# Weights of the FFN built piece by piece inside chunk 0, and the values of chunk 1 emptied by DVE: an attention and FFN layer on eight cores

## The chip, the cores and the metric

The kernel runs on one Trainium2 chip, with the same program on all 8 of its cores. Each core takes 4 of the 32 batch entries, and the cores exchange nothing. The time is that of the slowest core in device microseconds, and a figure for a kernel is the median of its runs.

## The reference, cut to what matters

```python
xn = layernorm(x)                                # x: 32 x 2048 x 1024
q1, q2, k1, k2 = (xn @ W.T for W in (W1_q, W2_q, W1_k, W2_k))   # 16 heads x 4
L_q, L_k = exterior(q1, q2), exterior(k1, k2)    # 6 products per head, unit norm
scores = (L_q @ (L_k @ J6.T).T) * 6 ** -0.5      # causal, softmax over the keys
out = softmax(scores) @ (xn @ W_v.T + b_v)       # 16 heads x 64
attn = out @ W_out.T + b_out
W_real = einsum('abcd,cefg->abefdg', G1_R, G2_R).reshape(512, 512)   # 4 terms
W_imag = einsum('abcd,cefg->abefdg', G1_I, G2_I).reshape(512, 512)
ffn = [x_re @ W_real.T - x_im @ W_imag.T, x_re @ W_imag.T + x_im @ W_real.T] + bias
return x + attn + ffn                            # x_re, x_im: the halves of xn
```

## The kernel before

A core has 8192 rows of x: 64 tiles of 128 rows, 4 tiles to a chunk, 16 chunks, 4 chunks to a batch entry. All engines run their instructions in the order of the program, which is written out by this Python code, so the place of a call is the place in every queue that it touches.

**Start-up (L707 to L741).** Tiles 0 to 3 are normalised and transposed on PE, their query and key products are made, then `v_unit(t, 0, True)` makes the first half of their values. A `v_unit` (L409) is 32 matmuls into the one bank F (L281), and then an eviction of F: with `by_act` true by ACT (L423), otherwise by DVE (L430). `evicted` (L285) notes who frees F and calls `background()`. For tiles 4 to 7 the layernorm comes in pieces from `ln_pipeline` (L672): `first` is the statistics on DVE (L212, L213), `second` is 1/std on ACT (L220, L222) with the statistics of the next tile, `third` is the application on DVE (L229), which in the start-up is followed by the transposes on PE (L245) and a copy by ACT (L256). One `background()` call stands ahead of the second halves of the values, `v_unit(t, 1, True)`, and each of these four calls it again when it has evicted.

**Background work.** Three queues hold pieces: `ext` (exterior products and norms of a new chunk's queries and keys: L338 to L380 on DVE, with `rsqrt` on ACT, L361), `lns` (the layernorm two chunks ahead) and `ffn`. The last has 24 pieces, `ffn_pieces` (L512): for each of 8 blocks of the FFN weights `products` (L519), `pairs` (L526) and `total` (L532, in the imaginary half with the negated copy L536). The one `background()` makes `pieces_at_once` rounds, and a round takes a piece of the first non-empty queue of `ext`, `lns`, `ffn`, in that order; a piece that puts nothing on DVE lets the round go on to the next queue. `pieces_at_once` is 2 at the end of the start-up, 3 in chunk 0 and 1 after it. Applying layernorm off PE sends a DMA transpose and the load of a later tile through SP's queue (L238, L207), and the last exterior piece four DMA transposes (L393, L396).

**The loop over chunks (L841).** A chunk's steps are pairs of a head group (4 of 4 heads) and a key tile `kt`; chunk 0 has 16 steps, each with `scores` on PE (L596), `exps` on ACT (L607), for diagonal tiles a `mask` on DVE (L617), and two steps later `sums` on PE (L635). A head group ends with `reciprocals` on ACT (L646, L648) and `normalize` on DVE (L656). Between them `Fillers.work` runs units on PE up to a quota: in chunk 0 two `qk_unit`s and eight `v_unit`s of chunk 1, each of 8 work units, and then `bias_unit` (L542, 32 matmuls of L559 in two halves; it makes the constant `outb`, L570, then loads the residual tiles 0 and 1, to which GpSimd adds `outb`, L451). In later chunks there are `out_unit`s (L491) too, the first users of the FFN weights: they make the FFN and the output projection of the chunk before, and DVE adds F to the residual (L483). All these units share bank F, so each waits for the eviction of the one before. At the end of a chunk what is left of `ext`, `lns` and `ffn` is issued in one go.

Of the kernel before, what the change touches and what calls it, by code (L numbers as in the profile page):

```python
# [19 lines left out]
CH = 4  # L20
# [37 lines left out]
def build(nb=NB):  # L58
# [22 lines left out]
    with st:  # L81
# [74 lines left out]
        xb_in = {}  # L156
# [3 lines left out]
        def wait_for(eng, token):  # L160
            if token is not None:
                token[0].wait(eng, token[1])
# [122 lines left out]
        def evicted(token):  # L285

            f_free[0] = token
            background()
# [190 lines left out]
        def out_add(t, half, bank):  # L479
            tS.wait(VE, tS.n)  # L480
            gS.wait(VE, xb_in[t])
            r = residual(t)[:, half * 512:half * 512 + 512]
            return vS.inc(VE.tensor_tensor(r, bank, r, OP.add))  # L483

        def store(t, half):

            cols = slice(0, 1024) if half is None else slice(half * 512, half * 512 + 512)
            vS.wait(SY, vS.n)
            y_out[t] = d_y[t % 2].inc(SY.dma_start(y_d[t * 128:(t + 1) * 128, cols], residual(t)[:, cols]), 16)

        def out_unit(t, half):  # L491
            wait_for(TE, f_free[0])
            yield from out_products(t, half, F, range(4), True)
            n = out_add(t, half, F[:])
            if half == 1:
                store(t, None)
                if t + 2 < NT - CH or t + 4 == NT - 1:
                    later.append(lambda: load_xb(t + (2 if t + 2 < NT - CH else 4)))
            evicted((vS, n))
# [12 lines left out]
        def ffn_pieces(ri, j):  # L512


            w = (wr, wi)[ri][:, j * 512:(j + 1) * 512]

            def products():
                d_g2.wait(VE, d_g2.n)
                vS.inc(VE.tensor_tensor(fview(TERM, [[512, 4], [16, 32], [1, 16]]),  # L519
                                        fview(G1O + (ri * 4 + j) * 128, [[32, 4], [1, 32], [0, 16]]),  # L520
                                        fview(G2O + ri * 64, [[16, 4], [0, 32], [1, 16]]), OP.mult))
                return True

            def pairs():
                vS.wait(VE, vS.n)
                vS.inc(VE.tensor_tensor(fview(TERM + 2048, [[1, 1024]]), fview(TERM, [[1, 1024]]),  # L526
                                        fview(TERM + 1024, [[1, 1024]]), OP.add))
                return True

            def total():  # L530
                vS.wait(VE, vS.n)
                vS.inc(VE.tensor_tensor(w, fview(TERM + 2048, [[1, 512]]), fview(TERM + 2560, [[1, 512]]),  # L532
                                        OP.add))
                if ri == 1:
                    vS.wait(VE, vS.n)
                    vS.inc(VE.tensor_scalar(wn[:, j * 512:(j + 1) * 512], w, -1.0, None, OP.mult))  # L536
                ffn_in[0] = vS.n
                return True

            return [products, pairs, total]  # L540
# [39 lines left out]
        def in_pairs(c, kt):  # L580


            return c % NCH >= 2 and shape(c, kt) < 256
# [76 lines left out]
        ext = deque()  # L660
        lns = deque()
        ffn = deque()
        later = deque()
        pieces_at_once = [1]

        def background():
            for _ in range(pieces_at_once[0]):
                for lane in [lane for lane in (ext, lns, ffn) if lane]:
                    if lane.popleft()():
                        break  # L670

        def ln_pipeline(tiles, on_pe=False):  # L672

# [49 lines left out]
            for _ in v_unit(t, 0, True):  # L723
                pass
        features[-1]()
        pieces_at_once[0] = 2
        lns.extend(ln_pipeline(range(CH, 2 * CH), True))
        for ri in range(2):
            for j in range(4):
                ffn.extend(ffn_pieces(ri, j))  # L730
        background()
        for t in range(CH):
            for _ in v_unit(t, 1, True):
                pass
        while lns:
            background()
        for t in range(2 * CH, 2 * CH + 3):
            load_x(t)
        for k in range(3):
# [18 lines left out]
        class Fillers:  # L758
# [3 lines left out]
            def __init__(self, c):  # L762
                nxt, prev = c + 1, c - 1
                self.qk, self.vs, self.outs = deque(), deque(), deque()
                if nxt < NC:
                    self.qk.extend(Unit(qk_unit(nxt, p), 8.0) for p in range(2))
                    self.vs.extend(Unit(v_unit(nxt * CH + t, h, c == 0), 8.0) for t in range(CH) for h in range(2))
                if c == 0:
                    self.vs.append(Unit(bias_unit(), 32.0))
                else:  # L770
                    self.outs.extend(Unit(out_unit(prev * CH + t, h), 16.0)
                                     for t in range(CH) for h in range(2))
                if nxt == NC:
                    for t in range(NT - CH, NT):
                        n = len(early_groups(t))
                        self.outs.extend(Unit(early_unit(t, h), 8.0 + 2 * n, lambda n=n: (c, n - 1) in o_in)
                                         for h in range(2))
                self.now = None
                self.done = 0.0
                self.started = 0  # L780
                self.ends = 4
                self.cost = sum(u.left for q in (self.qk, self.vs, self.outs) for u in q)

            def choose(self, end):
                n = self.started
                self.started += 1
                if self.qk and not end and n != 1 and (n == 0 or n >= 5):
                    return self.qk.popleft()
                spare = len(self.outs) - self.ends
                if self.outs and not self.outs[0].ready():  # L790
                    return None
                if self.outs and (end or not self.vs or 16 * spare > 8 * len(self.vs)):
                    return self.outs.popleft()
                for q in (self.vs, self.qk, self.outs):
                    if q:
                        return q.popleft()
                return None
# [43 lines left out]
        for c in range(NC):  # L841
            w = c % NCH
            fill = Fillers(c)
            pieces_at_once[0] = 3 if c == 0 else 1
            if c == NC - 1:
                later.extend(lambda t=t: load_xb(t) for t in range(NT - CH, NT - 1))
            if c + 2 < NC:
                lns.extend(ln_pipeline(range((c + 2) * CH, (c + 3) * CH)))
            steps = [(g, kt) for g in range(4) for kt in range(4 * w + 4)]
            quota = quotas(c, steps, fill.cost)  # L850
            target = 0.0
            for k, (g, kt) in enumerate(steps):
                pairs = in_pairs(c, kt)
                due = pend.popleft() if len(pend) == 2 else None
                end = due is not None and last_of_group(due)
                scores(c, g, kt, 0, 2 if pairs else 4)
                mm = tS.n
                exps(i, c, kt, mm, 0, 2 if pairs or end else 4)
                if due is not None:
                    sums(*due)  # L860
                if end:
                    ended, r = tS.n, reciprocals()
                if pairs:
                    scores(c, g, kt, 2, 2)
                    mm = tS.n
                if pairs or end:
                    exps(i, c, kt, mm, 2, 2)
                if pend and pend[-1][3] >= 4 * (pend[-1][1] % NCH):
                    p = pend.pop()
                    pend.append(p[:4] + (mask(*p),))  # L870
                pend.append((i, c, g, kt, (sS, sS.n)))
                target += quota[k]
                if end:
                    normalize(due[1], due[2], ended, r)
                    fill.ends -= 1
                    fill.work(max(target, fill.done + 12.0), True)
                else:
                    fill.work(target, False, 8.0 if kt == 0 else 3.0)
                if later and (k % 2 == 1 or w == 0):
                    later.popleft()()  # L880
                i += 1
            fill.rest()
            for lane in (ext, lns, ffn):
                while lane:
                    lane.popleft()()
            while later:
                later.popleft()()
# [53 lines left out]
```

How the kernel before makes its waits and increments, by code:

```python
    def inc(self, instr, k=1):  # L36
        instr.then_inc(self.h, k)
        self.n += k
        return self.n
# [1 line left out]
    def wait(self, eng, n):  # L41
        if n > self.had.get(id(eng), 0):
            eng.wait_ge(self.h, n)
            self.had[id(eng)] = n
```

## Time and profile before

| | us |
|---|---|
| median of 3 runs | 1771.18 |
| lowest, highest run | 1768.63, 1957.53 |
| profiled execution, its own time | 1771.96 |
| its span (core 1, the slowest) | 1770.9 |
| spans of the eight cores | 1757.7 to 1770.9 |
| PE busy, share of the span | 1582.8, 89% |
| ACT busy | 1210.7, 68% |
| DVE busy | 718.1, 41% |
| POOL (GpSimd) busy | 172.5, 10% |

A span runs from a core's first to its last instruction. Lines such as L519 are lines of the kernel before. A busy share is an average: the run has a start-up of 66 us, chunk 0 up to 154 us, and 15 chunks after it, and they have different limits.

### The profile page before, as it was taken

The page shows a single profiled execution, that of the slowest core. Times are in us where ns is not written, and L with a number is a line of the kernel's source. Part 1 is how long each engine was busy: PE and PEld are TensorE (multiplying, and loading weights), DVE is VectorE, ACT ScalarE, POOL GpSimd, SP SyncE. Part 2 cuts the span into 40 slices and gives each one's busy share as a digit, 9 for nine tenths or more (in the row PEclk, how much of TensorE's full clock was granted, in tenths as well). Part 3 has the DMA queues.
Part 4 walks back from the last instruction along what each step waited for, and adds up shares of the span by engine and source line. Part 5 has one row for each costly group of instructions (what it writes and reads, how often), then busy time and mean ns, then how long its engine had stood idle before and what let it go on. Part 6 is the DMA issues. An engine that isn't in the chain of part 4 may idle for free.

```text
span 1770.9 us, 57248 instructions; the slowest of 8 cores (1757.7 to 1770.9 us)
## 1 busy us (share of the span) xinstructions
PE 1582.8 (89%) x24704; PEld 621.0 (35%) x24704; DVE 718.1 (41%) x1343; ACT 1210.7 (68%) x1408; POOL 172.5 (10%) x142
## 2 busy tenths in 40 slices
PE   3657999999988999999988999999997899999998
PEld 2323433333334443333334443333333443333332
DVE  5577534233245543333235553332226554321112
ACT  2434767878853668788774567878883466778786
POOL 1001110100011111000011110110001111012000
PEclk9978989999999999999999999999999999999999
DMA  9421522313235251321223442341223533122101
GB/s 203 97 74 38 117 65 64 88 55 68 73 79 133 73 145 38 97 61 37 75 83 103 122 109 71 75 103 37 56 61 91 145 79 79 38 62 85 38 25 49
DMA packets 159064, 141.20 MB, mean 80 GB/s; under 512 B 128224, under 2 KB 132448, under 8 KB 158816
## 3 DMA queue, kind: packets, MB, share of 16 engines
q1 hardware_dynamic: 154432, 132.75, 29.2%
q0 software_dynamic: 4384, 4.78, 1.8%
q8 instruction: 199, 3.26, 0.8%
q14 instruction: 49, 0.40, 0.1%
HBM read 78.32 MB, written 33.55 MB: 63 GB/s over the span
## 4 chain that ended last, share of the span: by engine, by line
PE 69%; DVE 11%; ACT 11%; issue 6%; DMA 2%; SPq 0%; DVEq 0%; ACTq 0%; POOL 0%; POOLq 0%
PE F L281 34%; PE S L596 14%; PE OA L635 8%; ACT ex L607 8%; PE DN L635 5%; PE OB L635 5%; DVE oT L656 3%; DVE xb L483 2%; DMA wqk<-wqkT 1%; DVE vt L430 1%; ACT rden L648 1%; ACT rden L646 1%; DVE qks L304 1%; DVE vt L519 1%; PE F L559 1%
## 5 line engine op out<-in xcount | busy, mean ns | idle before, releaser
L607 ACT ACTIVATE ex<-S 128x1024 bf16<-128x1024 f32 (+4 forms) x1055 | 1082.3, 1049 | 457.9 <-PE S L596 443.8
L596 PE MATMUL S<-fq,fk 6*128 6x512 bf16 (+3 forms) x2560 | 378.3, 357 | 42.7 <-ACT ex L607 40.4
L451 POOL TENSOR_TENSOR xb<-xb,outb 128x512 f32<-128x512 f32 x122 | 157.3, 1310 | 1506.9 <-DMA xb<-x 1506.9
L281 PE MATMUL F<-wv,xnT 128*32 128x512 bf16 x4096 | 265.1, 388 | 25.2 <-ACT vt L423 12.3
L281 PE MATMUL F<-wo,oT 128*32 128x512 bf16 x4024 | 268.0, 386 | 6.5 <-DVE oT L656 6.5
L635 PE MATMUL OA<-ex,vt 128*32 128x512 bf16 (+3 forms) x2560 | 238.9, 363 | 33.6 <-DVE ex L617 18.1
L596 PEld LDWEIGHTS S<-fq,fk 6*128 6x128 bf16 x2560 | 101.0, 91 | 453.3 <-issue 449.2
L635 PE MATMUL DN<-ex,ones 128*32 128x512 bf16 (+3 forms) x2560 | 235.1, 356 | 0.0
L483 DVE TENSOR_TENSOR xb<-F,xb 128x512 f32<-128x512 f32 x122 | 84.4, 691 | 370.3 <-PE F L281 356.1
L635 PE MATMUL OB<-ex,vt 128*32 128x512 bf16 (+3 forms) x2560 | 234.1, 355 | 0.0
L617 DVE TENSOR_TENSOR ex<-ex,tri 128x512 bf16<-128x512 bf16 x256 | 104.3, 419 | 232.2 <-ACT ex L607 231.7
L430 DVE CAST vt<-F 128x512 bf16<-128x512 f32 x112 | 77.5, 692 | 210.9 <-PE F L281 210.9
L281 PE MATMUL F<-wr,xnT 128*32 128x512 bf16 x2048 | 144.3, 383 | 15.5 <-DVE qks L305 9.3
L281 PEld LDWEIGHTS F<-wv,xnT 128*32 128x32 bf16 x4096 | 102.4, 97 | 143.2 <-issue 77.2
L281 PEld LDWEIGHTS F<-wo,oT 128*32 128x32 bf16 x4024 | 105.6, 97 | 114.2 <-issue 30.9
L635 PEld LDWEIGHTS OA<-ex,vt 128*32 128x32 bf16 x2560 | 67.1, 93 | 163.3 <-issue 152.1
L635 PEld LDWEIGHTS DN<-ex,ones 128*32 128x32 bf16 x2560 | 70.1, 99 | 54.8 <-issue 4.1
L281 PE MATMUL F<-wi,xnT 128*32 128x512 bf16 x1024 | 73.2, 382 | 13.7 <-DVE xb L483 13.5
L281 PEld LDWEIGHTS F<-wr,xnT 128*32 128x32 bf16 x2048 | 49.7, 96 | 68.6 <-issue 39.3
L281 PE MATMUL F<-wqk,xnT 128*32 128x256 bf16 x1984 | 65.5, 281 | 9.2 <-DVE vt L430 5.0
L656 DVE TENSOR_TENSOR oT<-OA,rden 128x512 bf16<-128x512 f32 x64 | 44.1, 689 | 65.6 <-ACT rden L648 65.6
L281 PE MATMUL F<-wn,xnT 128*32 128x512 bf16 x1024 | 69.2, 383 | 0.2 <-issue 0.2
(77 smaller groups left out, 844.2 us busy)
## 6 DMA issues: line engine op xcount, KB each, us to landing
xst<-x SPq DMA_DIRECT2D x62, 512.0 KB, 4.6
xb<-x SPq DMA_DIRECT2D x61, 512.0 KB, 4.3
y<-xb SPq DMA_DIRECT2D x60, 512.0 KB, 3.0
wv<-wvT POOLq DMA_DIRECT2D x4, 512.0 KB, 30.2
wo<-woP POOLq DMA_DIRECT2D x4, 512.0 KB, 39.4
ex<-x SPq DMA_DIRECT2D x3, 512.0 KB, 11.0
y<-xst SPq DMA_DIRECT2D x6, 256.0 KB, 2.2
oT<-x SPq DMA_DIRECT2D x2, 512.0 KB, 16.5
```

The lines of the kernel that those rows point to most:

```text
L281: ins = TE.matmul(bank[32 * j:32 * j + 32, lo:hi], stationary[:, 32 * j:32 * j + 32], moving, start=start, stop=stop, tile_position=(0, 32 ...
L304: vS.inc(VE.tensor_copy(view(qks, 0, [[96, 8], [1, 64]]), view(bank, 0, [[64, 8], [1, 64]])))
L430: v_in[t, half] = (vS, vS.inc(VE.tensor_copy(vt[:, o:o + 512], F[:])))
L451: gS.inc(GE.tensor_tensor(r[:, h * 512:(h + 1) * 512], r[:, h * 512:(h + 1) * 512], outb[:, h * 512:(h + 1) * 512], OP.add))
L483: return vS.inc(VE.tensor_tensor(r, bank, r, OP.add))
L519: vS.inc(VE.tensor_tensor(fview(TERM, [[512, 4], [16, 32], [1, 16]]), fview(G1O + (ri * 4 + j) * 128, [[32, 4], [1, 32], [0, 16]]), fview( ...
L559: ins = TE.matmul(F[:], vt[:, 18 * 1024 + k * 128:18 * 1024 + k * 128 + 128], wo[:, (k % 8) * 1024 + half * 512:(k % 8) * 1024 + half * 51 ...
L596: ins = TE.matmul(S[:, m * 512 + off:(m + 1) * 512], fk[32 * m:32 * m + 6, o:o + 128], fq[c % 2][32 * m:32 * m + 6, g * 512 + off:(g + 1) ...
L607: n = sS.inc(SE.activation(view(ex[i % 3], m0 * 512 + off, dims), view(S, m0 * 512 + off, dims), AF.Exp, scale=SCALE))
L617: return (vS, vS.inc(VE.tensor_tensor(blk, blk, view(tri, 0, [[0, 4], [1, 128]]), OP.mult)))
L635: ins = TE.matmul(acc[32 * m:32 * m + 32, off:512], ones[:, 0:32] if part == 2 else vt[:, o:o + 32], e[:, m * 512 + off:(m + 1) * 512], st ...
L656: vS.inc(VE.tensor_tensor(oT[c % 2][:, o:o + 512], acc[:], rden[:], OP.mult))
```

## The change

1. `background()` is rewritten. While FFN pieces are left, and in any case before chunk 1, a call takes one piece from each of the queues, now in the order `ext`, `ffn`, `lns`. Otherwise it stops at the first piece that uses DVE, as before. `pieces_at_once` goes.
2. Ahead of the second value halves in the start-up one layernorm piece is issued in place of two, and each of the four calls `background()` twice. The 24 FFN pieces are put into their queue only after that.
3. Each step of a chunk calls `background()` at its start as long as FFN pieces are left.
4. The eight `v_unit`s of chunk 1 are evicted by DVE (L430) and not by ACT (L423).
5. An `out_unit` isn't chosen until the FFN pieces are issued; FFN pieces left at the end of chunk 0 would go on into chunk 1.
6. `out_unit` first issues residual loads that are still queued, if its tile isn't among those issued.

```diff
         def out_unit(t, half):
+            while t not in xb_in:
+                later.popleft()()
             wait_for(TE, f_free[0])
...
-        pieces_at_once = [1]
+        begun = [False]
 
         def background():
-            for _ in range(pieces_at_once[0]):
-                for lane in [lane for lane in (ext, lns, ffn) if lane]:
-                    if lane.popleft()():
-                        break
+
+            every = bool(ffn) or not begun[0]
+            for lane in [lane for lane in (ext, ffn, lns) if lane]:
+                if lane.popleft()() and not every:
+                    break
...
         features[-1]()
-        pieces_at_once[0] = 2
         lns.extend(ln_pipeline(range(CH, 2 * CH), True))
-        for ri in range(2):
-            for j in range(4):
-                ffn.extend(ffn_pieces(ri, j))
         background()
         for t in range(CH):
             for _ in v_unit(t, 1, True):
                 pass
+            background()
         while lns:
             background()
+        for ri in range(2):
+            for j in range(4):
+                ffn.extend(ffn_pieces(ri, j))
...
-                    self.vs.extend(Unit(v_unit(nxt * CH + t, h, c == 0), 8.0) for t in range(CH) for h in range(2))
+                    self.vs.extend(Unit(v_unit(nxt * CH + t, h), 8.0) for t in range(CH) for h in range(2))
...
-                    self.outs.extend(Unit(out_unit(prev * CH + t, h), 16.0)
+                    self.outs.extend(Unit(out_unit(prev * CH + t, h), 16.0, lambda: not ffn)
...
-                if self.outs and not self.outs[0].ready():
-                    return None
-                if self.outs and (end or not self.vs or 16 * spare > 8 * len(self.vs)):
+                ready = self.outs and self.outs[0].ready()
+                if ready and (end or not self.vs or 16 * spare > 8 * len(self.vs)):
                     return self.outs.popleft()
-                for q in (self.vs, self.qk, self.outs):
+                for q in (self.vs, self.qk, self.outs if ready else None):
...
-            pieces_at_once[0] = 3 if c == 0 else 1
+            begun[0] = c > 0
...
                 pairs = in_pairs(c, kt)
+                if ffn:
+                    background()
                 due = pend.popleft() if len(pend) == 2 else None
...
+            while ffn and c > 0:
+                ffn.popleft()()
             fill.rest()
-            for lane in (ext, lns, ffn):
+            for lane in (ext, lns):
                 while lane:
                     lane.popleft()()
```

## Rows read from the trace of the kernel before

**Rows 1.** Sums by stretch of core 1; its first row names the columns.

```profile
core 1: us, PE busy (x) PEld busy (x) DVE busy (x) ACT busy (x) POOL busy (x), PEclk, DMA share, GB/s
46.00:65.60 19.60, 13.35 (x224) 6.81 (x216) 9.48 (x12) 11.11 (x22) 0.00 (x0) 1.00 0.43 95
65.60:154.20 88.60, 53.28 (x744) 23.23 (x744) 63.63 (x100) 33.32 (x48) 0.14 (x1) 0.80 0.28 71
...
400.00:500.00 100.00, 95.42 (x1344) 32.51 (x1346) 28.90 (x57) 87.23 (x104) 7.51 (x6) 1.00 0.30 68
```

**Rows 2.** PE's timeline, chunk 0: start, us, work, [idle before <-releaser].

```profile
92.13 3.60 PE L281 MATMUL F<-wv,xnT 128*32 128x512 bf16 x32 [7.38 <-ACT vt L423]
...
126.32 1.87 PE L559 MATMUL F<-wo,vt 128*128 128x512 bf16 x4 [6.18 <-DVE vt L550]
...
137.59 2.18 PE L559 MATMUL F<-wo,vt 128*128 128x512 bf16 x7 [3.60 <-DVE outb L570]
...
153.30 0.30 PE L635 MATMUL OA<-ex,vt 128*32 128x128 bf16 x4 [5.22 <-DVE ex L617]
```

**Rows 3.** PE's timeline in the start-up: values (x32), transposes (x8), first scores.

```profile
54.30 1.91 PE L281 MATMUL F<-wv,xnT 128*32 128x512 bf16 x32
57.03 0.61 PE L245 MATMUL S<-tri,xnb 128*128 128x128 bf16 x8 [0.82 <-DVE xnb L229]
57.57 1.91 PE L281 MATMUL F<-wv,xnT 128*32 128x512 bf16 x32
...
63.72 0.61 PE L245 MATMUL S<-tri,xnb 128*128 128x128 bf16 x8 [0.89 <-DVE xnb L229]
65.59 0.40 PE L596 MATMUL S<-fq,fk 6*128 6x512 bf16 x4 [1.26 <-ACT xnT L256]
```

**Rows 4.** ACT's timeline in the start-up, around the eviction of values.

```profile
52.49 0.58 ACT L423 ACTIVATE vt<-F 128x512 bf16<-128x512 f32 x1
...
55.39 0.28 ACT L220 ACTIVATE stat<-stat,cvec 128x1 f32<-128x1 f32 x1
55.77 0.20 ACT L222 ACTIVATE stat<-stat 128x1 f32<-128x1 f32 x1
56.33 0.60 ACT L423 ACTIVATE vt<-F 128x512 bf16<-128x512 f32 x1 [0.35 <-PE F L281]
```

**Rows 5.** DVE's sum in one stretch: us, busy (instructions), clock, DMA, GB/s.

```profile
63.50:153.10 89.60, 63.94 (x100) 0.80 0.27 65
```

**Rows 6.** The page's costliest groups: the eviction of values by DVE.

```profile
L430 DVE CAST vt<-F 128x512 bf16<-128x512 f32 x112 | 77.5, 692 | 210.9 <-PE F L281 210.9
```

**Rows 7.** DVE's waits in the same stretch: us in total, times, longest.

```profile
DVE qks L304 <- PE F L281: 5.9, 2, 3.1
DVE stat L212 <- DMA xst<-x: 5.8, 1, 5.8
DVE ex L617 <- ACT ex L607: 4.4, 1, 4.4
DVE oT L656 <- ACT rden L648: 4.3, 2, 3.5
DVE outb L570 <- PE F L559: 1.4, 1, 1.4
DVE xnb L229 <- ACT stat L222: 0.3, 1, 0.3
```

**Rows 8.** DVE's timeline: an FFN piece, exterior products, a bias addition.

```profile
60.14 2.29 DVE L519 TENSOR_TENSOR vt<-vt 128x2048 f32<-128x2048 f32 x1
...
69.37 0.35 DVE L339 TENSOR_TENSOR ub<-qks 128x192 f32<-128x192 f32 x1
...
144.88 0.69 DVE L570 TENSOR_TENSOR outb<-F,outb 128x512 f32<-128x512 f32 x1 [1.43 <-PE F L559]
...
154.19 1.35 DVE L338 TENSOR_TENSOR ua<-qks 128x192 f32<-128x192 f32 x1
```

**Rows 9.** GpSimd's timeline: the residual additions of tiles 0 and 1.

```profile
154.06 5.31 POOL L451 TENSOR_TENSOR xb<-xb,outb 128x512 f32<-128x512 f32 x4 [127.71 <-DMA xb<-x]
```

## Prediction

> **What bounds the kernel now.** I began with the sums by stretch. In a steady stretch PE is busy 95.4 of 100 us at a granted clock of 1.00, the upper of its two levels (2.4 GHz), and DVE 28.9 [rows 1]. No edit reaches that part: once the FFN queue is empty and chunk 1 has begun, `background` stops at the first DVE piece as before, the values were DVE's there already. In the last chunk, where units aren't ready, the other queues are empty, so the new `choose` also returns nothing. So all that can move lies ahead of the first `out_unit`, and from there a delay passes on to the end nearly one to one. That part takes 88.6 us of chunk 0 (65.6 to 154.2), in which PE is busy 53.3 us at a mean clock of 0.80, ACT 33.3 and DVE 63.6 [rows 1]. PE can't be the bound there; its timeline names it. PE waits 7.38 us for ACT's eviction, 6.18 for the constant of `bias_unit` behind FFN pieces on DVE, 3.60 for the addition to `outb`, and 5.22 for a mask that stands behind the FFN pieces issued at the end of the chunk [rows 2]. Last, DVE's own waits show that it isn't simply full: 22.1 us in all, of which 5.8 for a tile of x, and ACT's rstd, then its eviction, stood behind that same statistics instruction [rows 7].
>
> **Part 1, the start-up: +5.4 us.** Before, 1/std of a tile stands on ACT ahead of the eviction of the value unit in front of it. Afterwards ACT's order is eviction, 1/std, copy; so transposition, next value products, eviction, 1/std and application form one chain. Its links: transposition to products 0.54 (57.03 to 57.57), products to eviction 2.03 (54.30 to 56.33), eviction 0.60, 1/std to the next transposition 1.64 (55.39 to 57.03): 4.81 us a tile [rows 3, 4]. Before it was (63.72 - 57.03) / 2 = 3.35 [rows 3]. The first transposition comes at 52.49 + 0.58 + 1.64 = 54.7, the last three periods later at 69.1 in place of 63.72: 5.4 us late. Nothing hides it, since the first scores wait for the copy of that tile (65.59) [rows 3]. A shift of 5.4 holds for the end of the last application on DVE too, which I put at 63.5: DVE is free from 68.9.
>
> **Part 2, chunk 0, as a ledger of DVE.** Steps call `background` 16 times at most and evictions 12 times. The 24 FFN pieces go one to a call, so the last is issued at the start of step 13 of 16; layernorm (9 pieces) and the exterior pieces go beside them. I wrote down DVE's order call by call: the pieces (up to 2.29 us, `products` [rows 8]) stand ahead of masks and evictions, PE then waits for DVE nearly everywhere up to step 13, and DVE for nobody. So DVE's busy time counts there. From 63.5 to 153.1 it was busy 63.9 us in 100 instructions [rows 5]. Added: one `products` of 2.29 us that was done earlier, at 60.14, in the start-up [rows 8], and eight evictions of 0.692, that is 5.5 us [rows 6]. (The one `pairs` of the start-up lies inside the stretch.) Gaps between dependent instructions remain: 89.6 - 63.9 = 25.7 us idle, less 22.1 of waits, is 3.6 [rows 5, 7]. Work and gaps: 63.9 + 2.3 + 5.5 + 3.6 = 75.3 us.
>
> Waits come back in the tail, where no FFN piece is left: 3.5 us for ACT's `rden`, as the longest before [rows 7]; the second half of the bias, 144.88 - 137.59 = 7.3 us [rows 2, 8] less some 1.5 of masks and an addition, 5.8; chunk 1's query products, 2.2 (the longest wait for them was 3.1 [rows 7]); some 0.5 for an exp: 12.0 together. The copy of chunk 1's first queries, at 153.1 before, then comes at 68.9 + 75.3 + 12.0 = 156.2: **+3.1 us**. So chunk 0 is 2.3 us shorter than before, although three of PE's stalls go: the 7.38 (the eviction is no longer behind 1/std, and x arrives before it is asked for, as its load is issued some 8 us ahead), the 6.18 and the 5.22. They turn into shorter waits for DVE at each step.
>
> The eviction price is taken from rows alone: 0.69 on DVE, 0.58 to 0.60 on ACT [rows 4, 6]. The Trainium skill, "VectorE: DVE Perf Modes", Specifications, says that ScalarE sits closer to PSUM and VectorE closer to SBUF; this speaks against edit 4, and the rows agree in size, 0.1 us apiece.
>
> **Part 3, GpSimd's addition: -1.5 us.** In `bias_unit` the first residual loads wait for everything that DVE had been given when the half ended, FFN pieces too. They landed so that GpSimd added from 154.06 for 5.31 us [rows 9], exactly while DVE did the four exterior products: 1.35 us in place of 0.35 [rows 8], some 4 us in all. Afterwards the loads go right after the last bias addition, about 154, and the addition starts near 158, when three of the four products are over. The gain lies between 0 (they still meet) and 4.2; I take 1.5. The Trainium skill, "SBUF — State Buffer", Who interferes with whom, has the rule: a DVE instruction with two SBUF inputs and a GpSimd instruction that reads SBUF exclude each other. The trace agrees, and it would put the gain at the upper end if they miss each other.
>
> **Nothing** for the others: `later` is never needed in `out_unit` (each tile was issued before its use already), readiness is true from chunk 1 on, and SP's transposes and loads stay the same in number. ACT loses 8 × 0.60 = 4.8 us of work in a stretch where it is busy 33.3 of 88.6 [rows 1].
>
> **Sum.** 3.1 - 1.5 = +1.6 us on the profiled execution's own 1771.96: 1773.6, rounded 1774. The median of the runs is 0.8 below that execution, so this may read 0.8 high.
>
> **The rivals.**
> *The stalls simply go.* DVE packs its work into its 22.1 us of waits, PE gets 7.4 + 6.2 + 5.2 = 18.8 us back, less the 5.4 of the start-up: 1758.6. For it: DVE's idle time [rows 7] is as large. Against: 7.8 us of new work and a tail that has to follow PE; DVE would have to end at 142, after 68.9 + 75.3 = 144.2.
> *The lower clock and DVE's waits stay.* With PE waiting at every step, the granted clock stays near 1.2 GHz, 32 products take 3.60 us and not 1.91 [rows 2, 3], and DVE has to wait for them. If it waits as much as before, 22.1 and not 12.0, and GpSimd still collides: 3.1 + 10.1 = +13.2, 1785.
> *Slower by over 2%.* The pieces at the head of each step stand ahead of the mask, sums and the next eviction, and nothing overlaps. PE's 53.3 us and DVE's 75.3 in a row are 128.6, 40 us longer than chunk 0 was, with the start-up +45: 1817. It decides from the point where DVE waits over 44 us in the stretch (12 + 35.4 - 3.1), about four per value unit. Against: products of 1.9 to 3.6 us run beside pieces that don't need them.
>
> **How the numbers follow.** The forecast has a chance of 0.6 (own range 1768 to 1779), the stalls that go 0.13, the lower clock 0.24, over 2% slower 0.03. The range goes from 1763 to 1786: below, the forecast with GpSimd's full gain and the tail's waits halved (3.1 - 4.2 - 6.0 = -7.1, 1765) and a little of the first rival; above, the second. What is left out is the first rival's own value and the last rival. Two per cent, about what a measurement of this kernel tells from no change, is 35 us. Only the last rival reaches it, and the first falls well short: faster 0.01, same 0.96, slower 0.03.
>
> **What would show it.** In the changed kernel: transpositions 4.8 us apart and first scores near 71; DVE without a wait over 2 us between 70 and 138, FFN pieces spread up to step 13; PE's waits in chunk 0 many, of 1 to 4 us, for L430 and L617; the first `out_unit` at 156 to 158; GpSimd's first addition 3 to 4 us later. It would be wrong if DVE waited longer for PE or ACT than 12 us in chunk 0, if x came late again, or if the steady part itself moved.

## The result: 0.5% slower, and the profile after

| | before | changed |
|---|---|---|
| median of 5 runs, us | 1768.63 | 1777.41 |
| lowest run | 1768.38 | 1776.33 |
| ratio, with its 95% interval | | 1.0048 [1.0032, 1.0064] |
| profiled execution, its own time | 1771.96 | 1778.67 |
| spans of the eight cores | 1757.7 to 1770.9 | 1765.3 to 1777.6 |
| first scores, median of the 8 cores | 65.9 | 76.3 |
| first `out_unit`, median of the 8 cores | 155.2 | 169.3 |

Single executions scatter by some 5 us, and the slowest core isn't always the same one. The program has a second, slower state in some executions, and the ratios and the figures per core leave these out. So the tables below also use a steadier figure: each core's median span over the runs, averaged over the eight cores ("mean core"). It is 1770.2 for the changed kernel; for the kernel before it is 1758.5, measured with the first experiments. The position of the first scores and of the first `out_unit` comes from the profiled execution, as a median of eight cores, and "chunk 0" is the median of their distances. They are one execution each: the cores of one profile differ by 4 us and more in them. The mean core and the ratio, which goes by the slowest core, can disagree by some 4 us.

Three stretches of the changed kernel, core 7, the slowest (busy us, instructions in brackets; PEclk is the granted clock):

```profile
core 7: us, PE busy (x) PEld busy (x) DVE busy (x) ACT busy (x) POOL busy (x), PEclk, DMA share, GB/s
46.00:65.60 19.60, 13.93 (x180) 6.25 (x172) 4.43 (x8) 7.30 (x15) 0.00 (x0) 0.83 0.47 105
65.60:154.20 88.60, 53.10 (x648) 22.13 (x648) 67.76 (x100) 27.45 (x42) 0.00 (x0) 0.75 0.25 60
...
400.00:500.00 100.00, 95.91 (x1364) 32.98 (x1364) 30.03 (x60) 86.14 (x103) 7.51 (x6) 1.00 0.27 68
```

The steady stretch is as in [rows 1]: PE 95.91 of 100 us at clock 1.00. The start-up is not. Its clock was 1.00 before and is 0.83 now, with PE busy nearly as long (13.93 against 13.35 us) for fewer matmuls (180 against 224). Over the eight cores that clock lies between 0.68 and 0.91, where it was 1.00 on all of them. DVE has 4.43 us of work there in place of 9.48.

PE's timeline in the start-up of the changed kernel, the lines that answer to [rows 3]:

```profile
56.13 2.94 PE L281 MATMUL F<-wv,xnT 128*32 128x512 bf16 x32
61.33 0.73 PE L245 MATMUL S<-tri,xnb 128*128 128x128 bf16 x8 [2.26 <-DVE xnb L229]
61.99 3.42 PE L281 MATMUL F<-wv,xnT 128*32 128x512 bf16 x32
67.73 0.61 PE L245 MATMUL S<-tri,xnb 128*128 128x128 bf16 x8 [2.33 <-DVE xnb L229]
...
74.01 0.61 PE L245 MATMUL S<-tri,xnb 128*128 128x128 bf16 x8 [2.31 <-DVE xnb L229]
75.88 0.62 PE L598 MATMUL S<-fq,fk 6*128 6x512 bf16 x4 [1.26 <-ACT xnT L256]
```

The transpositions (L245, x8) stand 6.3 us apart (67.73 to 74.01) where they stood 3.35, and the value products between them take 3.42 us for the same 32 matmuls that took 1.91. PE waits 2.3 us for DVE's `xnb` at each tile. ACT's timeline of the same stretch, as in [rows 4], now begins with the eviction and has 1/std behind it:

```profile
59.19 0.60 ACT L423 ACTIVATE vt<-F 128x512 bf16<-128x512 f32 x1 [1.87 <-PE F L281]
59.68 0.29 ACT L220 ACTIVATE stat<-stat,cvec 128x1 f32<-128x1 f32 x1
60.06 0.20 ACT L222 ACTIVATE stat<-stat 128x1 f32<-128x1 f32 x1
```

DVE over the ledger's stretch of the changed kernel, from the end of the last start-up application to the copy of chunk 1's first queries, as in [rows 5]; and its waits, as in [rows 7]:

```profile
73.86:167.60 93.74, 71.10 (x108) 0.76 0.24 57
```

```profile
DVE ex L619 <- ACT ex L609: 6.3, 2, 4.5
DVE xnb L229 <- ACT stat L222: 5.5, 1, 5.5
DVE vt L430 <- PE F L281: 3.7, 3, 2.4
DVE qks L304 <- PE F L281: 2.6, 1, 2.6
DVE oT L658 <- ACT rden L650: 2.5, 1, 2.5
DVE outb L572 <- PE F L561: 1.6, 1, 1.6
```

(The 5.5 us for `xnb` end at 73.05, ahead of the stretch.) DVE is busy 71.10 of 93.7 us. Named waits are 16.7 us and 2.0 more just before the copy at 167.63.

Six of PE's nine waits of over 2 us in chunk 0, as in [rows 2]:

```profile
103.39 0.41 PE L637 MATMUL OA<-ex,vt 128*32 128x256 bf16 x4 [3.70 <-DVE ex L619]
...
112.73 3.51 PE L281 MATMUL F<-wv,xnT 128*32 128x512 bf16 x32 [2.69 <-DVE vt L430]
...
129.69 0.24 PE L637 MATMUL OA<-ex,vt 128*32 128x128 bf16 x4 [4.14 <-DVE ex L619]
...
136.21 1.41 PE L281 MATMUL F<-wv,xnT 128*32 128x512 bf16 x16 [2.52 <-DVE vt L430]
...
147.06 1.86 PE L561 MATMUL F<-wo,vt 128*128 128x512 bf16 x4 [5.59 <-DVE vt L552]
...
157.30 3.14 PE L561 MATMUL F<-wo,vt 128*128 128x512 bf16 x7 [3.60 <-DVE outb L572]
```

The 7.38 us stall is gone, and so is the one of 5.22 at the end of the chunk. The wait for the bias constant is 5.59 (6.18 before). What came in their place are seven waits of 2.1 to 4.1 us, five for a mask (L619) and two for an eviction by DVE (L430).

### The profile page after: what moved, and what is told of

Same layout as the page of the kernel before. It is cut to its first block, busy times and chain, and to the rows that moved or that the text cites. A ratio compares the mean times of both kernels' runs of the same rounds, so it can differ in the third digit from the quotient of the medians.

```text
span 1777.6 us, 57246 instructions; the slowest of 8 cores (1765.3 to 1777.6 us)
## 1 busy us (share of the span) xinstructions
PE 1591.6 (90%) x24704; PEld 626.1 (35%) x24704; DVE 711.4 (40%) x1351; ACT 1206.8 (68%) x1400; POOL 171.7 (10%) x142
## 4 chain that ended last, share of the span: by engine, by line
PE 72%; ACT 10%; DVE 10%; issue 6%; DMA 1%; DVEq 0%; ACTq 0%; POOL 0%; POOLq 0%
PE F L281 38%; PE S L598 15%; PE OA L637 8%; ACT ex L609 8%; PE DN L637 5%; PE OB L637 5%; DVE oT L658 2%; DVE xb L483 2%; DVE vt L430 1%; DMA wqk<-wqkT 1%; ACT rden L650 1%; ACT rden L648 1%; DVE qks L304 1%; DVE vt L521 1%; PE F L561 1%
## 5 line engine op out<-in xcount | busy, mean ns | idle before, releaser
L281 PE MATMUL F<-wv,xnT 128*32 128x512 bf16 x4096 | 274.3, 399 | 21.4 <-DVE vt L430 10.0
L619 DVE TENSOR_TENSOR ex<-ex,tri 128x512 bf16<-128x512 bf16 x256 | 106.8, 428 | 232.5 <-ACT ex L609 232.2
L430 DVE CAST vt<-F 128x512 bf16<-128x512 f32 x120 | 82.9, 691 | 210.1 <-PE F L281 208.2
## 6 DMA issues: line engine op xcount, KB each, us to landing
ex<-x SPq DMA_DIRECT2D x3, 512.0 KB, 12.4
```

Of the source, the lines that this page charges most:

```text
L281: ins = TE.matmul(bank[32 * j:32 * j + 32, lo:hi], stationary[:, 32 * j:32 * j + 32], moving, start=start, stop=stop, tile_position=(0, 32 ...
L430: v_in[t, half] = (vS, vS.inc(VE.tensor_copy(vt[:, o:o + 512], F[:])))
L619: return (vS, vS.inc(VE.tensor_tensor(blk, blk, view(tri, 0, [[0, 4], [1, 128]]), OP.mult)))
```

## The experiments

Two theories stood at the start. Theory 1: the loss is the start-up's chain, lengthened by the lower clock that its waits bring. Theory 2: it is in chunk 0, by DVE's evictions and the call of `background` at each step. Ratios are to the kernel before, measured on the same chip, with their 95% intervals; where "mean core, before" is empty there was no such figure beside it.

| kernel | ratio | mean core, before | mean core, this | first scores | first out_unit | chunk 0 |
|---|---|---|---|---|---|---|
| before | 1 | | 1758.5 | 65.9 | 155.2 | 89.2 |
| changed | 1.0048 [1.0032, 1.0064] | | 1770.2 | 76.3 | 169.3 | 93.0 |
| changed again | 1.0064 [1.0034, 1.0094] | 1758.6 | 1767.5 | 74.5 | 168.4 | 94.0 |
| changed, old start-up | 1.0003 [0.9977, 1.0030] | 1758.5 | 1757.5 | 64.6 | 158.1 | 93.0 |
| before, new start-up | 1.0085 [1.0053, 1.0117] | 1758.5 | 1770.3 | 74.8 | 167.7 | 93.4 |
| changed, PE kept busy in the start-up | 1.0022 [1.0006, 1.0039] | 1758.5 | 1762.0 | 70.1 | 161.6 | 91.7 |
| changed, ACT evicts | 1.0030 [1.0009, 1.0051] | 1758.5 | 1760.6 | 74.6 | 159.2 | 85.0 |
| before, DVE evicts | 1.0023 [0.9999, 1.0048] | 1758.6 | 1759.8 | 65.7 | 158.2 | 93.2 |
| order alone | 0.9974 [0.9948, 1.0000] | 1758.6 | 1749.9 | 64.5 | 148.3 | 83.8 |
| before, residual loads early | 1.0014 [0.9990, 1.0039] | 1758.6 | 1761.0 | 64.8 | 159.3 | 93.8 |
| order alone, five pieces early | 0.9971 [0.9947, 0.9994] | 1757.4 | 1753.2 | 72.5 | 150.5 | 78.0 |
| changed, old start-up, PE busy in chunk 0 | 1.0052 [1.0032, 1.0071] | 1757.4 | 1767.9 | 66.4 | 165.8 | 99.2 |
| order alone, again | 0.9957 [0.9932, 0.9983] | 1759.9 | 1749.7 | 64.6 | 149.0 | 84.1 |
| five pieces early, inputs first | 0.9925 [0.9897, 0.9952] | 1759.9 | 1745.7 | 65.7 | 144.9 | 78.2 |

### The start-up undone, and the start-up alone

```diff
 # changed kernel, old start-up
         background()
+        background()
         for t in range(CH):
             for _ in v_unit(t, 1, True):
```

> The changed kernel with the start-up order of before: two layernorm pieces ahead of the second value halves, then two after each, so that 1/std stands ahead of the eviction again. Theory 1 (the loss is the start-up chain, lengthened by the lower clock that its waits bring): transpositions 3.3 us apart, first scores near 66 in place of 75.9, granted clock 1.00 in 46 to 65.6, time 9 to 11 us below the changed kernel, so about 1767, level with before. Theory 2 (the loss is in chunk 0, by the evictions on DVE and a background call at each step): first scores near 66, but the first out_unit stays 10 us or more late against before and the time is within 3 us of the changed kernel's 1777.

The mean core fell to 1757.5, level with before, and the first scores came at 64.6. So the layernorm order of the start-up is worth the whole loss. That isn't the same as being its only cause: edit 4 alone is worth nearly as much, as shown below, and the new order of the pieces gives something back. And theory 1 had no room for the other half of this run: its first `out_unit` is still 3 us later than before, since chunk 0 takes 93.0 us and not 89.2.

```diff
 # kernel before, new start-up
-        pieces_at_once[0] = 2
+        pieces_at_once[0] = 1
...
         for t in range(CH):
             for _ in v_unit(t, 1, True):
                 pass
+            background()
```

> The kernel before with only the start-up's order changed (one piece ahead of the second value halves, two calls of one piece after each); chunk 0 is as before. Theory 1: transpositions 6.3 us apart, first scores near 75.5, time 9 to 11 us above before, 1778 to 1780. Theory 2: first scores late too, but chunk 0 takes it back in DVE's waits, within 3 us of before.

The same loss from the other side: +11.8 us of mean core, first scores at 74.8, 8.9 us late. Its chunk 0 wasn't "as before" either: it takes 93.4 us, 4.2 more, which neither theory had. On core 7 PE's first query products of chunk 0 take 3.17 us in place of 1.93, and DVE's copy waits 5.9 us for them in place of 3.1; so the start-up's clock reaches into chunk 0. The start-up row of core 7 in this kernel has the lower clock too, 0.85:

```profile
46.00:65.60 19.60, 13.45 (x184) 6.57 (x188) 5.42 (x11) 7.76 (x15) 0.00 (x0) 0.85 0.37 91
```

Theory 2, that chunk 0 makes it good or is itself to blame for the whole, falls with these two. That DVE's evictions cost time in chunk 0 doesn't fall with it.

### Is it the chain or the clock?

```diff
 # changed kernel, in the start-up
             for _ in v_unit(t, 1, True):
                 pass
+            for k in range(12):
+                TE.matmul(OB[:, 0:256], wv[:, k % 8 * 128:k % 8 * 128 + 128], wv[:, 0:256], start=True, stop=True)
             background()
```

> The changed kernel with 12 extra matmuls of 256 columns into a free bank after each of the four second value halves of the start-up, where PE waits 2.3 us anyway; their results aren't used. If the lower clock makes the 6.3 us period: clock 1.00, value products 1.91 us and not 3.42, period 4.8 to 5.0, first scores near 71, time 4 to 5 us below the changed kernel. If the period is set by ACT and DVE alone: still 6.3 us, or longer by the extra matmuls (+1 us a tile).

PE's timeline in the start-up of this kernel, core 1; L735 is the extra work:

```profile
59.54 1.91 PE L281 MATMUL F<-wv,xnT 128*32 128x512 bf16 x32
61.39 1.48 PE L735 MATMUL OB<-wv 128*128 128x256 bf16 x12
63.77 0.61 PE L245 MATMUL S<-tri,xnb 128*128 128x128 bf16 x8 [0.90 <-DVE xnb L229]
...
68.54 0.61 PE L245 MATMUL S<-tri,xnb 128*128 128x128 bf16 x8 [0.90 <-DVE xnb L229]
70.41 0.40 PE L598 MATMUL S<-fq,fk 6*128 6x512 bf16 x4 [1.26 <-ACT xnT L256]
```

The products take 1.91 us again, the period is 4.77 us (63.77 to 68.54), and the clock of the stretch was 1.00, on all eight cores. The first scores come at 70.1, 4.4 to 6.2 us ahead of the changed kernel's two profiles, and the mean core is 1762.0, 5.5 below the changed kernel's second measurement and 8.2 below its first. So PE's waits of 2.3 us brought the granted clock down, and the clock lengthened the very products that the chain waits for. The changed kernel's own profile agrees: where a tile's products still took 1.91 us, the next transposition came 4.70 us after the last (cores 5 and 6), and where they took 3.60, 6.9 us (cores 0 and 3). Against the old start-up 5.5 us remain (70.1 - 64.6), against the kernel before 4.2 (70.1 - 65.9). That is the chain itself, at the upper clock: the period of 4.81 us and the 5.4 us of the prediction.

### Who evicts, and in which order of pieces

```diff
 # changed kernel, ACT evicts (in the kernel before, DVE evicts: the reverse)
-Unit(v_unit(nxt * CH + t, h), 8.0)
+Unit(v_unit(nxt * CH + t, h, c == 0), 8.0)
```

> The changed kernel with the eight value units of chunk 1 evicted by ACT as before. DVE's ledger: 8 x 0.61 = 4.9 us less work in a stretch in which DVE is the bound, so 3 to 5 us faster than the changed kernel. Rival: evictions then stand behind 1/std and rsqrt on ACT, which wait for DVE pieces that are now spread over all steps (ACT's waits for DVE were 11.5 and 10.4 us in the changed kernel): no gain or 3 us slower.

> The changed kernel itself, unaltered, on the chip of the runs beside it. Both theories: 9 to 12 us above before, first scores 75 to 77, first out_unit 168 to 170.

> The kernel before with only the eight value units of chunk 1 evicted by DVE. Theory 1 in its present form (an eviction on DVE makes DVE and PE wait for each other at each unit, beyond its own 0.69 us): first out_unit 4 to 8 us later than before, 6 us slower. Rival (the eviction costs its work alone, and ACT's evictions behind 1/std cost before as much as that): first out_unit within 3 us of before, since the 7.4 us wait for ACT's eviction goes.

> The changed kernel with the start-up order of before and the evictions by ACT: of the change only the FFN pieces one at a time, a call at each step, and the later queueing are left. If start-up and evictions are each to blame and add up: first scores 65 to 66, chunk 0 about 85 us long, first out_unit near 151, time 7 to 10 us below before. If they don't add up, because both cure the same lower clock in chunk 0: level with before, within 3 us.

With ACT's evictions the changed kernel's chunk 0 is 8.0 to 9.0 us shorter (85.0 against 93.0 and 94.0), about twice the 3 to 5 us that I had expected from the work alone; the rival fell. The time shows less of it: 9.6 or 6.9 us by the mean core against the changed kernel's two measurements, but with a ratio of 1.0030 it is still 5 us slower than before. In the order of before the same edit costs only 4.0 us of chunk 0, and in time 1.2 us of mean core or 4 by the ratio, whose interval reaches down to none. Its `out_unit` is 3 us late, at the edge of what the rival allowed; but the stall that the rival expected to go did not: PE waits up to 6.3 us for L430 where it waited 7.4 for ACT's eviction (core 1). "Order alone" is 8.7 and, measured again, 10.2 us of mean core faster than before, by the ratios 5 and 8 us, and the first interval just touches 1. The first of its two expectations held: start-up and evictions are each to blame. The lengths of chunk 0 (with the old start-up where there are both):

| | ACT evicts | DVE evicts |
|---|---|---|
| pieces in the order of before | 89.2 | 93.2 |
| pieces one at a time, a call at each step | 83.8, 84.1 | 93.0 |

So the new order of the FFN pieces is worth 5.2 us with ACT's evictions and nothing with DVE's, and DVE's evictions cost 4.0 us in the old order and 9.0 in the new. These two edits don't add up. DVE's waits in "order alone", core 1, from 63.5 to 147:

```profile
DVE ex L619 <- ACT ex L609: 6.4, 2, 4.5
DVE qks L304 <- PE F L281: 2.8, 2, 2.1
DVE oT L658 <- ACT rden L650: 2.5, 1, 2.5
DVE outb L572 <- PE F L561: 1.6, 1, 1.6
```

There is no line for `vt`, since DVE has no eviction there. The kernel beside it in the table, with DVE's evictions and the old start-up, has 3.9 us of it and 18.6 us of named waits in place of 13.3, and its PE waits 6.2 us for L430 where "order alone" waits 2.0 us for ACT (core 1 of both). With DVE full of pieces an eviction stands behind them. In the changed kernel, core 7:

```profile
111.91 0.68 DVE L430 CAST vt<-F 128x512 bf16<-128x512 f32 x1
...
116.36 0.69 DVE L430 CAST vt<-F 128x512 bf16<-128x512 f32 x1 [2.44 <-PE F L281]
```

The value products end at 110.04 and are evicted at 111.91, after a `products` piece of 2.28 us, a mask and the two instructions of `normalize`. PE waits for that, 2.69 us up to 112.73, as shown above; its next products take 3.51 us at the lower clock, and DVE waits 2.44 us for them.

> 'Order alone' again, as the neighbour of the next run: 7 to 9 us below before, first out_unit near 147.5.

The second measurement of "order alone" agrees: 0.9957 [0.9932, 0.9983], first `out_unit` at 149.0.

### Would PE's clock explain DVE's waits in chunk 0?

```diff
 # changed kernel, old start-up, ahead of chunk 0's scores
+                if c == 0:
+                    sS.wait(TE, max(s_free))
+                    for m in range(12):
+                        TE.matmul(S[:, m % 4 * 512:m % 4 * 512 + 256], wv[:, m % 8 * 128:m % 8 * 128 + 128],
+                                  wv[:, 0:256], start=True, stop=True)
```

> The changed kernel with the start-up order of before, and 12 extra matmuls of 256 columns (1.3 us at the upper clock, results not used) ahead of each of chunk 0's 16 scores. If the lower clock makes DVE wait for value products there: granted clock in chunk 0 near 0.9 to 1.0 in place of 0.75, DVE's waits for L430 gone (3.9 us), first out_unit 2 to 6 us earlier than 158.8 to 159.6. If DVE's order alone sets the length: 20 us more PE work, out_unit within 2 us. If PE's place in the chain counts more than its clock: 5 to 15 us later.

The stretch from first scores to first `out_unit`, core 7:

```profile
67.16:166.11 98.95, 74.01 (x926) 40.45 (x925) 68.82 (x107) 28.69 (x39) 0.00 (x0) 0.84 0.26 60
```

The clock rose only to 0.84, from 0.76 in that stretch of the kernel without them. DVE still waits 3.6 us for L430, and the `out_unit` comes 7.7 us later: the third expectation. Some 20 us of PE work that was meant to fill gaps lengthened chunk 0 by 6.2 us, so PE's place in the chain counts although PE is busy for only three quarters of the time in this kernel. How much a full clock alone would give there isn't shown by this run and stays open.

### GpSimd's addition moved on its own

```diff
 # kernel before, bias_unit
-                evicted((vS, vS.inc(VE.tensor_tensor(outb[:, cols], F[:], outb[:, cols], OP.add))))
-            outb_in[0] = vS.n
+                outb_in[0] = vS.inc(VE.tensor_tensor(outb[:, cols], F[:], outb[:, cols], OP.add))
+                evicted((vS, outb_in[0]))
```

> The kernel before, with the loads of residual tiles 0 and 1 waiting only for the constant outb and not for the FFN pieces issued after it. Nothing else moves. GpSimd's first addition then falls near 149 to 154 beside FFN pieces of two SBUF inputs. If the collision with the exterior products cost before 3 us: those products take 0.35 us again, but the FFN pieces meet the addition instead, so the first out_unit comes 0 to 4 us later and the time stays within 3 us. If nothing collides: 3 us faster.

GpSimd and DVE in this kernel, core 7:

```profile
152.86 6.39 POOL L451 TENSOR_TENSOR xb<-xb,outb 128x512 f32<-128x512 f32 x4 [126.37 <-DVE vt L519]
```

```profile
148.18 1.23 DVE L526 TENSOR_TENSOR vt<-vt 128x1024 f32<-128x1024 f32 x1
149.50 0.69 DVE L532 TENSOR_TENSOR wi<-vt 128x512 bf16<-128x512 f32 x1
...
152.90 2.30 DVE L526 TENSOR_TENSOR vt<-vt 128x1024 f32<-128x1024 f32 x1
155.30 1.56 DVE L532 TENSOR_TENSOR wi<-vt 128x512 bf16<-128x512 f32 x1
...
158.06 1.48 DVE L617 TENSOR_TENSOR ex<-ex,tri 128x512 bf16<-128x512 bf16 x1
...
160.85 0.35 DVE L339 TENSOR_TENSOR ub<-qks 128x192 f32<-128x192 f32 x1
```

```profile
159.69 0.30 PE L635 MATMUL OA<-ex,vt 128*32 128x128 bf16 x4 [9.10 <-DVE ex L617]
```

The same forms take 1.23 and 0.69 us before 152.86 and 2.30 and 1.56 after it, and a mask 1.48 where it took 0.42; once GpSimd is done, an exterior product is back at 0.35. The collision only moved. DVE loses 3.9 us to it (L526, L532, L536 and the mask), no more than the 4.2 us of before, but now ahead of the mask that PE waits for, and that wait became 9.10 us where it was 5.22. Chunk 0 is 4.6 us longer, the first `out_unit` 4.1 us late (0 to 4 were expected), the time 2.4 us of mean core above before, within the 3 us expected. So an earlier addition isn't a gain by itself; what it falls beside decides.

### Less work for DVE in chunk 0

```diff
 # order alone, five pieces early
         background()
+        background()
+        lead = [piece for ri in range(2) for j in range(4) for piece in ffn_pieces(ri, j)]
+        for piece in lead[:5]:
+            piece()
         for t in range(CH):
...
-        for ri in range(2):
-            for j in range(4):
-                ffn.extend(ffn_pieces(ri, j))
+        ffn.extend(lead[5:])
```

> The kernel of 'order alone' (start-up and ACT's evictions as before, FFN pieces one at a time, a call at each step) with the first five FFN pieces issued ahead of the second value halves, where DVE was idle for 7.4 us. If chunk 0 is bound by DVE's work: 2.3 + 1.3 + 0.8 + 2.3 + 1.3 = 8.0 us leave it, first scores 65 to 67, chunk 0 76 to 79 us long in place of 82 to 84, first out_unit near 142, another 5 to 7 us off, 13 to 16 below before. If PE and ACT set it by now: within 2 us of 'order alone', 8 us below before.

Chunk 0 became 78.0 us, as expected of a stretch bound by DVE's work. But the first scores came at 72.5, 8 us late and far from the 65 to 67 expected, and the whole was no better than "order alone". DVE's timeline in the start-up, core 7:

```profile
52.32 2.29 DVE L521 TENSOR_TENSOR vt<-vt 128x2048 f32<-128x2048 f32 x1 [6.69 <-DMA vt<-g2x]
...
60.19 0.81 DVE L229 TENSOR_SCALAR xnb<-ex,stat 128x1024 bf16<-128x1024 f32 x1
```

The first piece waited 6.69 us for the FFN's inputs, which land at 52.3, and the application of the next tile stood behind all five pieces. The idle time that I had seen there couldn't be used, since its data wasn't there.

```diff
 # five pieces early, inputs first
-        for t in range(2 * CH):
+        for t in range(CH):
             x_in[t] = (d_x0[t], d_x0[t].inc(SY.dma_start(early[t], x_d[t * 128:(t + 1) * 128, :]), 16))
...
+        for t in range(CH, 2 * CH):
+            x_in[t] = (d_x0[t], d_x0[t].inc(SY.dma_start(early[t], x_d[t * 128:(t + 1) * 128, :]), 16))
         d_c.inc(SY.dma_start(bvs[:], bv_d), 16)
```

> The kernel with five FFN pieces early, with the ten loads of the FFN's inputs put ahead of the loads of x tiles 4 to 7 in SP's queue, since DVE had waited 6.7 us for them. If their place in the queue made them late: they land before 45, first scores 65 to 67, chunk 0 77 to 78 us long, first out_unit near 143, 5 us below 'order alone'. If the DMA engines are simply full of weights until 50: still near 52, and x tiles 4 to 7 late too, first scores 73 or later, no gain over 'order alone'.

This is the fastest of all: 0.9925 [0.9897, 0.9952], 14.2 us of mean core below before, chunk 0 78.2 us. Against "order alone, again" beside it the gain is 4.0 us of mean core, and the two intervals overlap. It isn't clean: on seven cores the first scores come at 63.8 to 67.1, on core 7 at 72.9. There tile 4 of x was late in its turn:

```profile
46.68 0.69 DVE L214 BATCH_NORM_STATS2 stat<-ex 128x6 f32<-128x512 f32 x1 [6.41 <-DMA ex<-x]
...
50.63 2.27 DVE L523 TENSOR_TENSOR vt<-vt 128x2048 f32<-128x2048 f32 x1
```

DVE waited 6.4 us for x, and then the five pieces followed from 50.63 to 58.5. Both expectations hold in part. The place in the queue mattered: on the other cores the first piece starts at 43.0 to 45.0 us without a wait for its inputs. But the FFN's loads now delay x: DVE waits for it there too, 0.5 to 2.9 us.

## Why the prediction was right, and where its sum was off

I had forecast 1774 with a range of 1763 to 1786 and no change beyond 2%; it is 1777.41. The stretches that move and the bound of chunk 0, DVE's work, were right. The sizes of all three parts were off. The first two errors add up (5.0 and 6.1 us), and the third takes only 1.7 back:

| part | predicted | measured |
|---|---|---|
| 1, start-up: first scores | +5.4 | +10.4 (65.9 to 76.3) |
| 2, chunk 0 | -2.3 | +3.8 (89.2 to 93.0) |
| 3, after the first `out_unit` | -1.5 | -3.2 (-2.1 in the second profile) |
| sum | +1.6 | +11.0 |

The mean core says +11.7, the medians of the runs +8.8, and the profiled executions' own times +6.7. So that 1777.41 lies near 1774 is in part luck: the sum was 5 to 10 us too small, by which of these one takes, and what held was a range of 23 us that reached up to the second rival. By the prediction's own sign of being wrong, more than 12 us of DVE's waits in chunk 0, its part 2 was wrong.

**Part 1.** The step that failed is the link "products to eviction 2.03", taken from a stretch at clock 1.00; in the changed kernel it is 3.53 us (68.27 to 71.80 on core 7). Its other links held: in the changed kernel an eviction is followed by 1/std 0.49 us later (59.19, 59.68) and PE waits 2.3 us for the application as it had to. With these waits the granted clock fell, the products took 3.42 us, and each tile 6.3 us in place of 4.81. I had given this effect to chunk 0 as a rival and not thought of it in the start-up. The run with extra matmuls shows the split: 4.2 to 5.5 us chain, and 4.4 to 6.2 us clock.

**Part 2.** The step that failed is "and DVE for nobody": DVE's waits ahead of the tail were put at nothing and came to 6.3 us. The ledger of DVE's work held: 63.9 + 2.3 + 5.5 = 71.7 us forecast, 71.10 measured, and gaps of 93.74 - 71.10 - 18.7 = 3.9 us (3.6). Of waits 12.0 us were forecast and 18.7 measured. The tail alone is nearly as predicted: 1.8 for an exp, 2.5 for `rden`, 4.5 + 1.6 around the second bias half and 2.0 for the queries are 12.4. What is missing stands ahead of it: 2.6 for chunk 1's first query product, which took 3.6 us at the lower clock, and 3.7 for three value products. The price of the evictions on DVE was then not 0.69 us each, 5.5 in all, but 1.1 us each where DVE is full: 9.0 us for eight, by the table above.

**Part 3.** The addition did move past the exterior products. GpSimd and DVE in the changed kernel, core 7:

```profile
170.45 4.97 POOL L451 TENSOR_TENSOR xb<-xb,outb 128x512 f32<-128x512 f32 x4 [143.77 <-DMA xb<-x]
```

```profile
167.63 0.69 DVE L304 COPY qks<-F 128x512 f32<-128x512 f32 x1 [1.97 <-PE F L281]
...
168.76 0.36 DVE L338 TENSOR_TENSOR ua<-qks 128x192 f32<-128x192 f32 x1
...
174.51 1.33 DVE L345 TENSOR_TENSOR ua<-ua,ub 128x384 f32<-128x384 f32 x1
```

The products take 0.36 us and only the subtraction L345 meets it (1.33 in place of 0.56). By the rule of the Trainium skill ("SBUF — State Buffer", Who interferes with whom) a DVE instruction with two SBUF inputs contends with a GpSimd instruction that reads SBUF, and these rows agree. 3.2 us were measured, from the first `out_unit` to the next value products (9.4 us before, 154.23 to 163.66; 6.2 after, 168.80 to 175.02). Most of it isn't GpSimd's: the first FFN products of chunk 1 found the lower clock before and the upper one after. PE in the kernel before, then in the changed one:

```profile
154.23 1.90 PE L281 MATMUL F<-wr,xnT 128*32 128x512 bf16 x16 [0.42 <-DVE qks L305]
...
160.94 0.40 PE L635 MATMUL OA<-ex,vt 128*32 128x512 bf16 x4 [1.23 <-DVE oT L656]
```

```profile
168.80 1.05 PE L281 MATMUL F<-wr,xnT 128*32 128x512 bf16 x16 [0.68 <-DVE qks L305]
```

1.90 against 1.05 us for the same 16 matmuls. The kernel with the early residual loads divides the two: its exterior products meet no addition, but its FFN products are at the lower clock (1.90), and the same distance is 8.2 us (160.62 to 168.86, core 7). So the collision was worth 1.2 us, near the 1.5 forecast and far from the 4.2 that DVE loses to it: PE waited behind it only 1.23 us, for `oT`. The other 2.0 are the clock's, and the prediction had no term for that. In the changed kernel's second profile the distance has a median of 7.4 us, so the clock's share is 0.9 to 2.0.

**The rivals.** "The stalls simply go" did happen in one sense: without edit 4 and the new start-up the order of the pieces gives 8.7 to 10.2 us of mean core, not far from its 13.4 (it had to end DVE's stretch 13.4 us earlier, so at 139.7, and not at 142 as it stands there). The changed kernel lost that to the other two edits. "The lower clock and DVE's waits stay" was the nearer one for the size, with 18.7 us of waits against its 22.1; but it looked for the loss in chunk 0 alone, where nearly half of the excess came in the start-up, and it had GpSimd's collision, which did not come. Slower by over 2% was far off.

## What to carry to other kernels

A chain that makes TensorE wait at each round lengthens itself, if what it waits for is TensorE's own work: take its links at both clocks before summing. Work moved to an engine that a stretch is bound by costs more than its duration, because whatever frees a single buffer then queues behind everything else there (1.1 us for an eviction of 0.69 here); spread background work over the steps, but leave the evictions with the engine that has room. And an idle stretch is only room if the inputs are there: look at when they land before moving work into it.

## What the runs showed of the hardware

- Four dozen matmuls with results that nobody uses, in waits of 2.3 us, brought a start-up's granted clock from 0.68 to 0.91 (the eight cores) back to 1.00 on all of them and shortened its period from 6.3 (core 7) to 4.8 us. In chunk 0, with waits of several us, 12 extra matmuls a step raised it only from 0.75 (cores 1 and 7 of the kernel without them, 65.6 to 154.2) to 0.87 and 0.84, and chunk 0 became 6.2 us longer.
- Beside GpSimd's float32 additions even the negated copy with one input (L536) took 1.17 us and not 0.29, and a bf16 mask 1.48 and not 0.42, in the kernel with the early residual loads.
